# Audio tower on one core: the token mixer's convolution of chunks one to three, interleaved in pairs of heads

## The chip, the cores and the metric

The kernel runs on one core of one Trainium2 chip. The metric is the device time of one launch in microseconds, lower is better. In the trace PE is TensorE (PEld its weight loads), DVE VectorE, ACT ScalarE, POOL GpSimd, SP SyncE.

## What is computed

A layer of an audio tower on 2,048 rows of 1,024 channels (32 sequences of 64 rows, after folding four steps of 256 channels into one row), in three parts. The change lies in the first, the token mixer:

```
h = xf @ W_proj + b_proj                 # 1024 x 1024
y = layernorm(h, ln_g, ln_b)
w = softmax((y @ W_wgen + b_wgen) by head over 5 taps)       # 8 heads
conv = sum over taps k of  w[.., k] * y shifted by 4-k rows  # per head, 128 channels
out = h + relu(conv @ W_ff + b_ff)
```

Then follow `h + attention(layernorm(h))` (8 heads of 64, causal) and `h + ffn(layernorm(h))` (16 heads, 64 to 256 to 64, with a permutation of channels).

## The kernel before

**Layout.** The rows (tokens) are the columns of work here, cut into CH = 4 chunks of N = 512. Channels lie on the 128 partitions in KB = 8 blocks; a chunk's block is 128x512. Every engine has its program written out by hand, and semaphores order the engines (`since(e, s, c, per, k)` waits until semaphore `s` has reached `c * per + k`). Each engine runs its program in order. All eight PSUM banks (128x512 f32 each) are in use.

**The feed-forward product** of chunk c, `conv @ W_ff`, is done by `ff_group(c, g, k)`: for the output blocks of group g (`A_GROUPS`: banks 0 1 2, then 3 4 5, then 6 7) and the input block k, three matmuls each (high and low halves: `split3`, lines 339 to 341). Group 2 is thus eight steps of six matmuls into banks 6 and 7. I call such a step G0 to G7.

**The convolution** of a chunk is done head by head, between those steps of the chunk ahead of it. `turn(n, h)` (T0 to T7) is four PE transposes of the head's y into bank 0 or 2, by h % 2 (line 1687). ACT copies it to SBUF (`turn_evac`, line 900), into one of two buffers. `conv(n, h)` (C0 to C7) is 32 small 64x64 matmuls with the head's band of tap weights (line 1706), into two banks. DVE prepares the band (`band_turn`, line 1320; two buffers). ACT takes the result's high part (`conv_high`, line 905), DVE the low part (`conv_low`, line 1326), which releases the banks. For chunks 1 to 3 every head uses the same two banks, 3 and 4, so `conv(n, h)` waits for the low part of head h-1 (`cv_lo`).

**PE's order in `b_step(c)`**, c = 0, 1, 2, after groups 0 and 1 of chunk c: T0 | G0 T1 C0 | G1 T2 C1 | ... | G6 T7 C6 | G7 C7, where G are of chunk c and T and C of chunk c + 1.

**Beside it, in chunk 1's convolution only** (c = 0), ACT squares the eight blocks of the last chunk's centred values for its layernorm, one square after each `conv_high` (line 364; S0 to S7). ACT's order there is: copy of T(h), high part of C(h-1), S(h). The squares have two buffers, and S(k) waits for POOL's variance addition k-2 (`ln_square_act` waits on `ln_vac`, for k from 2). POOL's order, written out by hand, is:

```
for m in range(3):
    b_add(0, m)
for k in range(1, 4):
    ln_var_add(g, CH - 1, k)
for m in range(3, 6):
    b_add(0, m)
for k in range(4, KB):
    ln_var_add(g, CH - 1, k)
```

`ln_var_add(k)` (line 375; V1 to V7) needs S(k). `b_add(0, m)` (line 768) adds the residual block m, which SP loads into two buffers: the load of block m + 2 is issued after addition m and its store (lines 581, 585).

Of the kernel before, what the change touches and what calls it, by code (L numbers as in the profile page):

```python
# [10 lines left out]
KB = D // P  # L11
# [22 lines left out]
def audio_tower(nc, x_t, w_proj, w_ff, w_gen, w_qkv_t, w_o_t, up, down, vecs, perm, *outs):  # L34
# [12 lines left out]
    with ctx:  # L47
# [5 lines left out]
        def sem(name):  # L53
            return ctx.enter_context(nc.semaphore(name))
# [140 lines left out]
        cv_mm, cv_hi, cv_lo, ff_mm, ff_ev, ff_add = (  # L195
            sem(s) for s in ("cv_mm", "cv_hi", "cv_lo", "ff_mm", "ff_ev", "ff_add"))
# [20 lines left out]
        def since(e, s, c, per, k):  # L217

            if isinstance(c, int):
                if c * per + k > 0:  # L220
                    e.wait_ge(s, c * per + k)
            else:
                e.wait_ge(s, c * per + k)
# [50 lines left out]
        def cv_out(n, h, s):  # L274

            return bank[cv_banks(n, h)[s]][:, 0:N // 2].rearrange("p (t q) -> p t q", q=SEQ)
# [73 lines left out]
        def ln_mean_pe(pe, L):  # L350
            since(pe, ln_sum, L, 7, 7)
            since(pe, ln_std, L - 1, 1, 1)
            pe.matmul(bank[LN_BANK][:, :], mean_w[:, :], acc[:, :], start=True, stop=True).then_inc(ln_mean, 1)
# [28 lines left out]
        def ln_var_pe(pe, L):  # L382
            since(pe, ln_vac, L, 7, 7)
            since(pe, ln_d, L, 8, 8)
            pe.matmul(bank[LN_BANK][:, :], mean_w[:, :], vacc[:, :], start=True, stop=True).then_inc(ln_var, 1)
# [1202 lines left out]
        def _(pe):  # L1588
# [62 lines left out]
            def gate_block(n, k):  # L1651
                since(pe, yr_lo, n, 8, k + 1)
                if k == 0 and n < CH - 1:
                    pe.wait_ge(a_ev, 8 * (n + 1))
                if k == 0 and n == CH - 1:
                    pe.wait_ge(ff_ev, 8)

                for whole in (True, False) if k == 0 else (False, True):
                    if whole:
                        mm = pe.matmul(bank[7][0:2 * LOGITS, :], wg[:, k, :, :], yr_h[:, k % 2, :],  # L1660
                                       start=k == 0, stop=k == KB - 1)
                    else:
                        mm = pe.matmul(bank[7][0:LOGITS, :], wg[:, k, 0, :], yr_l[:, k % 2, :],
                                       start=False, stop=False)
                mm.then_inc(yr_used, 1)

            def gate_turn(n):

                since(pe, lg_ev, n, 1, 1)
                for t in range(TILES):  # L1670
                    mm = pe.matmul(bank[7][:, t * LOGITS:(t + 1) * LOGITS],
                                   lg[:, t * P:(t + 1) * P], fold[0:2 * LOGITS, :], start=True, stop=True)
                mm.then_inc(lgt_mm, 1)

            def turn(n, h):

                pe.wait_ge(y_b, 8 * n + h + 1)
                if h < 2:
                    if n == 0:
                        pe.wait_ge(a_ev, 8 * (CH - 1) + YT_BANKS[1] + 1)  # L1680
                    else:
                        pe.wait_ge(ff_ev, 8 * (n - 1) + YT_BANKS[h] + 1)
                else:
                    pe.wait_ge(yt_ev, 8 * n + h - 1)
                y = db[n]
                for t in range(TILES):
                    mm = pe.transpose(bank[YT_BANKS[h % 2]][:, t * P:(t + 1) * P], y[:, h, t * P:(t + 1) * P],  # L1687
                                      ident[:, :])
                mm.then_inc(yt_mm, 1)

            def conv(n, h):
                if n == 0:
                    pe.wait_ge(a_ev, 8 * (CH - 1) + cv_banks(n, h)[1] + 1 + (h == 0))
                    since(pe, cv_lo, n, 8, h - 1)
                elif h == 0:
                    pe.wait_ge(ff_ev, 8 * (n - 1) + CV_BANKS[0][1] + 1)
                else:
                    pe.wait_ge(cv_lo, 8 * n + h)
                since(pe, yt_ev, n, 8, h + 1)
                since(pe, ar_ev, n, 8, h + 1)  # L1700
                halves = [slice(SEQ * i, SEQ * i + SEQ) for i in range(2)]
                for t in range(TILES):
                    for f in range(2):
                        col = t * P + f * SEQ
                        for s in range(2):
                            mm = pe.matmul(bank[cv_banks(n, h)[s]][halves[f], t * SEQ:(t + 1) * SEQ],  # L1706
                                           yt[halves[s], h % 2, col:col + SEQ],
                                           ar[halves[s], h % 2, t * SEQ:(t + 1) * SEQ], start=True, stop=True)
                mm.then_inc(cv_mm, 1)

            def ff_group(c, g, k):
                ms = A_GROUPS[g]
                if g == 0:
                    since(pe, cv_lo, c, 8, k + 1)
                if isinstance(c, int) and c == 0 and g < 2:
                    wait_units(pe, U_FF + KB * g + k + 1)
                for m in ms:
                    cols = slice(m * P, (m + 1) * P)
                    mm = split3(pe, bank[m][:, :], (wf_h[:, k, cols], wf_l[:, k, cols]),
                                (cv_h[:, k, :], cv_l[:, k, :]), k == 0, k == KB - 1)  # L1720
                    if k == KB - 1:
                        mm.then_inc(ff_mm, 1)
                if g == 2 and c == CH - 1 and k < KB - 1:
                    mm.then_inc(ff_used, 1)

            def b_step(c, ahead):


                LATE = CH - 1
                for i in range(2 * KB):  # L1730
                    if c == 0 and i == KB:
                        pe.wait_ge(mean3_ok, 1)
                    if c == 1 and i == 1:
                        pe.wait_ge(ff_ev, 8)
                        ln_var_pe(pe, LATE)
                    if not ahead and i == 2:
                        pe.wait_ge(ff_ev, 8 * (CH - 1))
                        ln_mean_pe(pe, CH)
                    if not ahead and i == 9:
                        ln_var_pe(pe, CH)  # L1740
                    ff_group(c, i // KB, i % KB)
                    if c == 1 and 0 <= i - 5 < KB:
                        gate_block(LATE, i - 5)
                    if c == 1 and i == 14:
                        gate_turn(LATE)
                if ahead:
                    turn(c + 1, 0)
                if c == 1:
                    pe.wait_ge(ln_std, CH)
                    pe.wait_ge(sm5, 8 * LATE + 1)  # L1750
                elif ahead:
                    pe.wait_ge(ff_ev, 8 * c)
                else:
                    pe.wait_ge(ln_std, CH + 1)
                for k in range(KB):
                    ff_group(c, 2, k)
                    if ahead:
                        if k + 1 < KB:
                            turn(c + 1, k + 1)
                        conv(c + 1, k)  # L1760


# [3 lines left out]
            for h in range(CONV_HEADS):  # L1766
                if h + 1 < CONV_HEADS:
                    turn(0, h + 1)
                conv(0, h)
                if h == MEAN_AFTER:  # L1770
                    stat_mean_pe(pe, CH - 1, MEAN_BANK)
            for c in range(CH - 1):
                b_step(c, True)
            b_step(CH - 1, False)


# [210 lines left out]
            for s in range(CH * KB):  # L1987
                c, a = divmod(s, KB)
# [14 lines left out]

A_GROUPS = [(0, 1, 2), (3, 4, 5), (6, 7)]

YT_BANKS, CV_BANKS = (0, 2), ((3, 4), (6, 7))

SMALL_AFTER, LOAD_AFTER, FIRST_LOW = 2, 4, 6

# [25 lines left out]

def cv_banks(n, h):

    return CV_BANKS[h % 2 if n == 0 else 0]


# [38 lines left out]
```

## Time and profile before

| | us |
|---|---|
| median of 3 runs | 966.39 (962.8 to 966.87) |
| the profiled execution: its time | 968.3 |
| its span, first to last instruction | 965.9 |
| mean granted TensorE clock | 0.991 of full |
| PE busy | 943.1 |
| chunk 1's convolution (T0 to the end of C7) | 256.9 to 278.1 |
| chunk 2's | 316.5 to 337.6 |
| chunk 3's | 370.4 to 391.5 |

A line of the timeline gives the start, the length (of the union, where several like instructions are merged, xN), the engine, the line of the kernel, the operation and its tiles, and in brackets the idle time of the engine before it with what released it. PE records overlap, because the matmuls are pipelined: how fast PE goes is read from the distance of starts, not from lengths.

### The profile page before, as it was taken

What the parts mean: (1) busy time and instruction counts of PE and PEld (TensorE: products, weight loads), DVE (VectorE), ACT (ScalarE), POOL (GpSimd) and SP (SyncE); (2) the same over time, 40 slices, a digit from 0 to 9 for tenths busy, and PEclk for the clock granted to TensorE, in tenths of its full rate; (3) what the DMA queues carried; (4) which work ended last, traced back from release to release, by engine and by line L of the source; (5) the groups of instructions that cost most, each with busy time, mean ns of one, the idle gap of its engine ahead of it and who ended that gap; (6) DMA issues with size and microseconds to landing.
All of it is one profiled execution on the core that took longest, in us unless ns stands there. A gap on an engine that the chain in (4) does not pass through costs nothing.

```text
span 965.9 us, 15776 instructions
## 1 busy us (share of the span) xinstructions
PE 943.1 (98%) x6108; PEld 707.5 (73%) x6108; DVE 540.3 (56%) x887; ACT 438.3 (45%) x774; POOL 387.6 (40%) x312
## 2 busy tenths in 40 slices
PE   9999999998999999999999999999999999999996
PEld 8778787776877788788778878878887766623342
DVE  5254544878658312356475266257064479788773
ACT  6244444482754543436253243244132232287874
POOL 1224242523752221823560550451023157487742
PEclk9999999999999999999999999999999999999999
DMA  7750605128354254149002002100124985634521
GB/s 259 279 177 1 224 1 211 33 92 257 115 181 125 88 150 161 45 160 336 5 12 99 22 12 61 60 13 23 42 79 143 259 302 201 260 116 137 170 105 76
DMA packets 54383, 122.99 MB, mean 127 GB/s; under 512 B 16283, under 2 KB 17307, under 8 KB 49830
## 3 DMA queue, kind: packets, MB, share of 16 engines
q1 hardware_dynamic: 49190, 105.22, 32.7%
q0 software_dynamic: 5120, 16.78, 5.1%
q8 instruction: 48, 0.79, 0.3%
q14 instruction: 25, 0.20, 0.1%
HBM read 79.37 MB, written 42.60 MB: 126 GB/s over the span
## 4 chain that ended last, share of the span: by engine, by line
PE 79%; DVE 6%; DMA 6%; issue 3%; POOL 2%; ACT 2%; SPq 1%; POOLq 0%; DVEq 0%; ACTq 0%
PE bank L339 20%; PE bank L341 19%; PE bank L340 19%; PE bank L1978 6%; PE bank L1962 3%; PE bank L1706 2%; DMA h<-h_s 2%; PE bank L1687 1%; DVE h L1489 1%; DVE sq L420 1%; DMA stage<-w_proj 1%; PE bank L1965 1%; DMA stage<-w_ff 1%; PE bank L1863 1%; PE bank L1836 1%
## 5 line engine op out<-in xcount | busy, mean ns | idle before, releaser
L375 POOL TENSOR_TENSOR vacc<-vacc,sq 128x512 f32<-128x512 f32 x72 | 97.4, 1353 | 44.9 <-ACT sq L425 33.3
L339 PE MATMUL bank<-cv_h,wf_h 128*128 128x512 f32 x256 | 105.2, 411 | 3.2 <-POOL wf_l L333 3.2
L339 PE MATMUL bank<-xa_h,wp_h 128*128 128x512 f32 x256 | 102.5, 400 | 0.1
L341 PE MATMUL bank<-cv_h,wf_l 128*128 128x512 f32 x256 | 100.5, 393 | 0.0
L340 PE MATMUL bank<-cv_l,wf_h 128*128 128x512 f32 x256 | 100.5, 392 | 0.0
L341 PE MATMUL bank<-xa_h,wp_l 128*128 128x512 f32 x256 | 100.4, 392 | 0.0
L340 PE MATMUL bank<-xa_l,wp_h 128*128 128x512 f32 x256 | 100.3, 392 | 0.0
L768 POOL TENSOR_TENSOR fo<-fo,res 128x512 f32<-128x512 f32 x32 | 44.1, 1392 | 100.2 <-ACT fo L910 75.2
L1170 ACT ACTIVATE gt<-bank 128x512 f32<-128x512 f32 x128 | 66.0, 603 | 33.6 <-PE bank L1962 20.1
L1978 PE MATMUL bank<-gt,dn_f 128*64 128x512 f32 x256 | 61.8, 604 | 0.0
L425 ACT ACTIVATE sq<-sq 128x512 f32<-128x512 f32 x56 | 34.6, 637 | 59.7 <-DVE sq L420 59.7
L1400 DVE TENSOR_SCALAR qk<-bank,vec 128x256 f32<-128x256 f32 x32 | 14.0, 480 | 84.1 <-PE bank L341 84.1
L339 PEld LDWEIGHTS bank<-cv_h,wf_h 128*128 128x128 f32 x256 | 48.4, 189 | 15.6 <-issue 4.5
L339 PE MATMUL bank<-vs_h,wo_h 128*128 128x512 f32 x128 | 53.1, 415 | 4.4 <-DVE vs_l L1449 4.0
L1326 DVE TENSOR_TENSOR cv_l<-bank,cv_h 128x256 fp32r<-128x256 f32 x64 | 24.2, 420 | 59.1 <-ACT cv_h L905 58.7
L403 POOL TENSOR_TENSOR acc<-acc,ho 128x512 f32<-128x512 f32 x24 | 33.6, 1399 | 58.9 <-ACT ho L881 56.6
L339 PEld LDWEIGHTS bank<-xa_h,wp_h 128*128 128x128 f32 x256 | 48.4, 189 | 11.9 <-issue 0.7
L340 PEld LDWEIGHTS bank<-xa_l,wp_h 128*128 128x128 f32 x256 | 48.5, 190 | 10.7 <-issue 0.7
L341 PEld LDWEIGHTS bank<-cv_h,wf_l 128*128 128x128 f32 x256 | 48.4, 189 | 10.5
L341 PEld LDWEIGHTS bank<-xa_h,wp_l 128*128 128x128 f32 x256 | 48.4, 189 | 10.4
L340 PEld LDWEIGHTS bank<-cv_l,wf_h 128*128 128x128 f32 x256 | 48.5, 190 | 10.1 <-issue 1.0
L833 POOL DMA_INDIRECT out<-hg,rows x32 | 37.3, 1165 | 42.1 <-DVE hg L1568 39.3
(194 smaller groups left out, 2240.2 us busy)
## 6 DMA issues: line engine op xcount, KB each, us to landing
xs<-x_t SPq DMA_DIRECT2D x32, 256.0 KB, 6.1
h_s<-ho SPq DMA_DIRECT2D x8, 1024.0 KB, 4.3
res<-h_s SPq DMA_DIRECT2D x32, 256.0 KB, 3.6
h_s<-fo SPq DMA_DIRECT2D x32, 256.0 KB, 2.5
dc<-h_s SPq DMA_DIRECT2D x4, 2048.0 KB, 9.0
h<-h_s SPq DMA_DIRECT2D x8, 1024.0 KB, 10.7
h_s<-h SPq DMA_DIRECT2D x8, 1024.0 KB, 6.1
band_s<-zero SPq DMA_DIRECT2D x4, 1096.0 KB, 8.5
```

The lines of the kernel that those rows point to most:

```text
L339: pe.matmul(o, wh, xh, start=start, stop=False)
L340: pe.matmul(o, wh, xl, start=False, stop=False)
L341: return pe.matmul(o, wl, xh, start=False, stop=stop)
L375: g.tensor_tensor(vacc[:, :], t[:, 0, :] if k == 1 else vacc[:, :], t[:, at, :], ALU.add).then_inc(ln_vac, 1)
L403: g.tensor_tensor(acc[:, :], blk(0) if k == 1 else acc[:, :], blk(k), ALU.add).then_inc(ln_sum, 1)
L425: act.activation(d, d, ACT.Square).then_inc(ln_sq, 1)
L768: g.tensor_tensor(fo[m % 4][:, :], fo[m % 4][:, :], res[:, m % 2, :], ALU.add).then_inc(ff_add, 1)
L833: g.indirect_dma_start(out=outs[c], out_offset=bass.IndirectOffsetOnAxis(ap=rows[:, k:k + 1], axis=0), in_=hg[c % 3][:, k, :], in_offset=N ...
L1170: act.activation(gt[a % 2][:, i, :], bank[i][:, :], ACT.Gelu).then_inc(gelu_ok, 1)
L1326: ins = v.tensor_tensor(one_seq(cv_l[:, h, :], s), cv_out(n, h, s), one_seq(cv_h[:, h, :].bitcast(F32), s), ALU.subtract)
L1962: mm = pe.matmul(bank[2 * blk + j][:, :], up_f[r, a, cols], dd[r, a, :], start=True, stop=True)
L1978: pe.matmul(bank[4 + a % 2][side, :], dn_f[:, FFB * a + 2 * head + blk, :], gt[a % 2][:, i, :], start=blk == 0, stop=blk == 1).then_inc(g_ ...
```

## The change

For chunks 1 to 3 the order in `b_step` becomes T0 T1 | G0 G1 T2 T3 C0 C1 | G2 G3 T4 T5 C2 C3 | G4 G5 T6 C4 C5 | G6 T7 C6 | G7 C7. Heads 1, 3 and 5 get banks 1 and 5 (free since group 2 writes only 6 and 7); the other heads keep 3 and 4. The waits of `conv` follow: C0 and C1 wait for the relu that empties their banks, C2 to C6 for the low part of head h-2, C7 for that of head 6. ACT's, DVE's, POOL's and SP's programs are unchanged.

```diff
@@ conv(n, h)
-                elif h == 0:
-                    pe.wait_ge(ff_ev, 8 * (n - 1) + CV_BANKS[0][1] + 1)
+                elif h < 2:
+                    pe.wait_ge(ff_ev, 8 * (n - 1) + cv_banks(n, h)[1] + 1)
+                elif h < 7:
+                    pe.wait_ge(cv_lo, 8 * n + h - 1)
                 else:
                     pe.wait_ge(cv_lo, 8 * n + h)
@@ b_step(c, ahead)
                 if ahead:
                     turn(c + 1, 0)
+                    turn(c + 1, 1)
...
                 for k in range(KB):
                     ff_group(c, 2, k)
-                    if ahead:
-                        if k + 1 < KB:
-                            turn(c + 1, k + 1)
+                    if ahead and k < 6 and k % 2:
+                        for h in (k + 1, k + 2):
+                            if h < 7:
+                                turn(c + 1, h)
+                        conv(c + 1, k - 1)
+                        conv(c + 1, k)
+                    if ahead and k == 6:
+                        turn(c + 1, 7)
+                    if ahead and k >= 6:
                         conv(c + 1, k)
@@ module level
-YT_BANKS, CV_BANKS = (0, 2), ((3, 4), (6, 7))
+YT_BANKS, CV_BANKS = (0, 2), ((3, 4), (6, 7), (1, 5))
@@ cv_banks(n, h)
-    return CV_BANKS[h % 2 if n == 0 else 0]
+    return CV_BANKS[h % 2 if n == 0 else 2 if h % 2 and h < 6 else 0]
```

## Rows read from the trace of the kernel before

**Rows 1.** The page: engines' busy time, and the chain that ended last.

```profile
PE 943.1 (98%) x6108; PEld 707.5 (73%) x6108; DVE 540.3 (56%) x887; ACT 438.3 (45%) x774; POOL 387.6 (40%) x312
...
PE 79%; DVE 6%; DMA 6%; issue 3%; POOL 2%; ACT 2%; SPq 1%; POOLq 0%; DVEq 0%; ACTq 0%
```

**Rows 2.** Timeline of PE, chunk 1's convolution (start, length, engine, line).

```profile
256.23 0.39 PE L339 MATMUL bank<-cv_h,wf_h 128*128 128x512 f32 x1
...
256.92 0.60 PE L1687 MATMUL bank<-ident,db_next 128*128 128x128 f32 x4
...
258.74 0.60 PE L1687 MATMUL bank<-ident,db_next 128*128 128x128 f32 x4
...
262.54 0.50 PE L339 MATMUL bank<-cv_h,wf_h 128*128 128x512 f32 x1
...
264.04 0.60 PE L1687 MATMUL bank<-ident,db_next 128*128 128x128 f32 x4
264.57 0.69 PE L1706 MATMUL bank<-ar,yt 64*64 64x64 f32 x32
265.19 0.50 PE L339 MATMUL bank<-cv_h,wf_h 128*128 128x512 f32 x1
...
277.46 0.69 PE L1706 MATMUL bank<-ar,yt 64*64 64x64 f32 x32
```

**Rows 3.** Timeline of PE, chunk 3's convolution: T1 and C7.

```profile
372.21 0.60 PE L1687 MATMUL bank<-ident,db_late 128*128 128x128 f32 x4
...
390.83 0.69 PE L1706 MATMUL bank<-ar,yt 64*64 64x64 f32 x32
```

**Rows 4.** Timeline of PE, chunk 0: T0 and T1 back to back.

```profile
206.58 1.03 PE L1687 MATMUL bank<-ident,db 128*128 128x128 f32 x8
```

**Rows 5.** Timeline of PE, attention: two sets of 32 small matmuls back to back.

```profile
497.14 0.69 PE L1863 MATMUL bank<-pt,vv 64*64 64x64 f32 x32
497.66 0.65 PE L1836 MATMUL bank<-qk 64*64 64x64 f32 x32
498.24 0.50 PE L339 MATMUL bank<-xc_h,wq_h 128*128 128x512 f32 x1
```

**Rows 6.** Timeline of ACT, POOL and DVE, chunk 1's convolution from S3 on.

```profile
265.87 0.64 ACT L364 ACTIVATE sq<-db_late 128x512 f32<-128x512 f32 x1
266.59 1.39 POOL L375 TENSOR_TENSOR vacc<-vacc,sq 128x512 f32<-128x512 f32 x1 [1.26 <-ACT sq L364]
267.93 2.73 POOL L768 TENSOR_TENSOR fo<-fo,res 128x512 f32<-128x512 f32 x2
272.61 1.28 POOL L768 TENSOR_TENSOR fo<-fo,res 128x512 f32<-128x512 f32 x1 [1.95 <-DMA res<-h_s]
273.85 5.59 POOL L375 TENSOR_TENSOR vacc<-vacc,sq 128x512 f32<-128x512 f32 x4
275.23 0.63 ACT L364 ACTIVATE sq<-db_late 128x512 f32<-128x512 f32 x1 [1.31 <-POOL vacc L375]
276.65 0.76 DVE L1326 TENSOR_TENSOR cv_l<-bank,cv_h 128x256 fp32r<-128x256 f32 x2 [1.25 <-ACT cv_h L905]
```

**Rows 7.** Timeline of PE: three gaps elsewhere in the kernel.

```profile
217.69 0.69 PE L1706 MATMUL bank<-ar,yt 64*64 64x64 f32 x32 [1.08 <-DVE ar L1320]
...
234.87 0.77 PE L339 MATMUL bank<-cv_h,wf_h 128*128 128x512 f32 x1 [3.17 <-POOL wf_l L333]
...
783.82 0.47 PE L339 MATMUL bank<-vs_h,wo_h 128*128 128x512 f32 x1 [1.90 <-DVE vs_l L1449]
```

**Rows 8.** Windows: engines' busy us (instructions), then granted PE clock, DMA share, GB/s.

```profile
216.00:220.00 4.00, 2.92 (x70) 2.15 (x71) 3.35 (x9) 2.46 (x7) 0.00 (x0) 1.00 0.20 66
234.00:239.00 5.00, 4.13 (x11) 3.31 (x12) 5.00 (x4) 1.28 (x3) 5.00 (x4) 0.66 0.97 217
784.00:788.00 4.00, 4.00 (x12) 3.11 (x11) 3.79 (x7) 0.31 (x1) 3.08 (x4) 0.57 0.64 186
```

**Rows 9.** Waits in total: POOL for residual loads (us, times, longest).

```profile
POOL fo L768 <- DMA res<-h_s: 25.0, 9, 6.6
```

## The prediction, made before the changed kernel was run

> **What bounds the kernel now.** I read the page first: PE is busy for 943.1 of 965.9 us, and the chain that ended last runs through PE for 79% of the span [rows 1]. So a microsecond taken from PE's own sequence counts, and a microsecond in which PE is made to wait counts too. Then I read PE's timeline through the three stretches that the diff touches. A plain matmul of a group is 0.23 us behind the one before it: three of them from 256.23 to T0 at 256.92. A full turn of the loop, from the first matmul of one G to that of the next, is 2.65 us (262.54 to 265.19), of which G is 1.50, T until C starts 0.53, and C until the next G 0.62. T0 with all of G0 behind it is 1.82 (256.92 to 258.74) [rows 2]. From T1 to C7 chunk 3 takes 18.62 us, seven turns of 2.65 and 0.07 for the way into C7: nothing waits there [rows 3]. In chunk 1 it is 18.72 (258.74 to 277.46) [rows 2], so C7 already waits 0.1 us. Last I read the other engines beside chunk 1, because only there ACT's squares stand in the same queue as the copies that PE needs.
>
> **What PE's sequence saves.** Per merged pair of heads, one change from T to C and one from C to G go away, and nothing is removed from the work.
> - *Two groups in a row:* the second has six matmuls at 0.23, 1.38 us, instead of 1.50. G G is 2.88.
> - *Two turns in a row:* eight transposes take 1.03 where four take 0.60 [rows 4, 2], so the second T costs 0.43, and T T is 0.53 + 0.43 = 0.96.
> - *Two products in a row:* no row of before shows C C. The nearest is attention, where a set of 32 small matmuls of the same tile follows another at once: 497.14 to 498.24, 1.10 us for both, against 0.62 for one [rows 5, 2]. The second costs 0.48. Its bounds are 0.62 (no gain: each C as dear as today) and 0.47, the start-to-start distance if nothing at all is lost. I take 0.48, since those rows have the same count and tile, other banks for the second set, and three waits ahead of it like C.
>
> A pair is 2.88 + 0.96 + 1.10 = 4.94 against 2 x 2.65 = 5.30: 0.36 saved (0.22 with the dear C). Three pairs are merged in each chunk: T2 T3 C0 C1; T4 T5 C2 C3; T6 C4 C5. T0 T1 ahead of G0 only moves 0.43 us from one place to another. So PE's sequence is 3 x 0.36 = 1.08 us shorter per chunk, 3.2 us in three (2.0 with the dear C).
>
> The Trainium skill ("TensorE: Matmul & The Clock Gate", the section on 56 ns against 53.3 ns) says that starts of matmuls never come closer than about 25 ns however small they are. By that floor 32 products would take 0.80 us, a second C would cost 0.80, and by an estimate from it a pair would save 0.04 us, 0.4 us in nine. The trace does not agree: 32 products and the way out take 0.62 [rows 2], so the rows decide.
>
> **Do the waits hold?** In chunks 2 and 3 ACT has only copies between the pairs, so yes: C(h) now waits for the low part of head h-2, a whole pair older, and T2 to T5 for copies made a pair earlier. Bank 5's relu is done before ACT copies T0, since it stands ahead of it in ACT's queue. C0 comes later than now, so DVE's bands are there. Both chunks get their 1.08 us.
>
> **Chunk 1 is another matter.** There every square S(h) stands behind the high part of C(h-1), and C2 moves. On PE: T0 256.92; T2 at +1.82 +0.43 +1.38 = 260.55; C0 +0.96 = 261.51; G2 +1.10 = 262.61; T4 +2.88 = 265.49; C2 +0.96 = 266.45. Today C2 is at 264.57: it comes 1.88 us later. What hangs on it today: S3 at 265.87 (1.30 behind C2), V3 at 266.59, the two residual additions 3 and 4 at 267.93, addition 5 at 272.61, which waited 1.95 us for a residual block whose load SP issues only after addition 3, then V4 to V7 from 273.85, 1.40 each, and S6 at 275.23, which stood 1.31 us waiting for V4 [rows 6]. Behind S6 in ACT's queue come the copy of T7 and the high part of C6, then DVE's low part, 276.65 to 277.41, then C7 at 277.46 [rows 6, 2]. Every link is back to back or a fixed latency, with no slack, apart from POOL's 1.26 us ahead of V3, which is itself the wait for S3. So the 1.88 us pass through to C7: 279.34.
>
> ACT can't take S6 earlier, and nothing that is behind it can pass. On PE, C7 would be due at: G4 266.45 + 1.10 = 267.55; T6 270.43; C4 270.96; G6 272.06; T7 273.56; C6 274.09; G7 274.71; C7 + 1.57 = 276.28. So PE stands still for about 3.0 us, with nothing to do: what is queued behind C7 is group 0 of chunk 1, which is not let past it. Chunk 1 ends 1.88 us later instead of 1.08 earlier.
>
> The earlier pairs of chunk 1 hold. From C0 at 261.51 ACT goes through the high part of C0, S1, copy of T2, high part of C1, S2, copy of T3 at about 0.54 each from 262.27 (S3 stands 1.30 behind its C and the high part 0.54 before it), so the copy of T3 ends near 265.6, and T5, which needs its bank, is due at 265.92.
>
> **The clock.** A gap of 3 us may cost more than its length. After the gap of 3.17 us ahead of 234.87 and that of 1.90 ahead of 783.82 the granted clock fell to its lower level (1.2 of 2.4 GHz): it was 0.66 over 234 to 239 and 0.57 over 784 to 788, which is 5 x 0.34 and 4 x 0.43, 1.7 us of full-rate work lost each time. After the gap of 1.08 ahead of 217.69 it stayed at 1.00 [rows 7, 8]. Mine is as long as those that fell, with dense matmuls ahead of it, so I take 1.7 (bounds 0 and 1.7).
>
> **Sum.** Chunk 1 +1.88 + 1.7, chunks 2 and 3 -2.16: +1.4 us. The later parts follow PE, whose gaps in them are waits for other engines that PE itself releases, so a shift passes on whole. Against the profiled execution, 968.3, that is 969.7; the median of the runs is 1.9 below the profiled one, so 966.4 + 1.4 = 967.8. A change of 0.5% (4.8 us) is about what this measurement can tell from none, and mine is 0.15%.
>
> **Rivals.**
> 1. *The stall is there, the clock holds.* For it: C7 and the work before are dense, and part of the half-rate stretch may fall into the gap itself. Against: both gaps of 1.9 us and more lost the full 1.7. Net +1.88 - 2.16 = -0.3: 966.1. Chance 0.2.
> 2. *No stall: the pairs give all they promise.* It would need the wait of addition 5 for its residual (1.95 us) or ACT's for V4 (1.31) to shrink by what C2 is later. For it: a load that is in flight alone may land sooner. Against: the load is issued by what it waits for. Then -3.2: 963.2, and with the dear C 964.4. Chance 0.14.
> 3. *Slower by more than can be missed.* The load of residual 5, issued between additions 3 and 4, may land much later than now, since it moves into other traffic. The longest wait of POOL for such a load is 6.6 us against 1.95 here [rows 9, 6]: C7 would be 4.65 later still, net +6.1: 972.5. It decides from a wait of 5.4 us on, where +4.8 is reached. Against: SP has nothing else in flight at that point. Chance 0.05.
> 4. *Small waits at each pair* (T5 misses its 0.3 us of margin, or a C waits for a band): 0.1 to 0.3 each, 967 to 969; inside the forecast's own width. The forecast with these has 0.61.
>
> **The numbers.** Forecast 967.8, its own range 966.5 to 969.5. Rivals 1 and 2 lie below it, so the range reaches down to 963.0; above it ends at 970.3, short of rival 3. Against no change (966.4): faster needs below 961.6, which no case reaches but for the scatter of the runs (962.8 to 966.9 before): 0.04. Slower needs above 971.2, rival 3 and scatter: 0.06. The same: 0.9.
>
> **What the profile after would show.** In chunks 2 and 3, from T0 to C7 19.4 us instead of 20.4, with C C 1.10 and T T 0.96: that proves the saving. In chunk 1, V3 near 268.5, S6 near 277.1 waiting for V4, a PE gap of about 3 us ahead of C7 near 279.3, put down to DVE's low part, and a granted clock below 1 behind it. C C at 1.24 would show the dear C. If C7 of chunk 1 starts near 276.3, the chain through POOL was wrong. If C7 is late but the clock stays at 1.00, only the price of the gap was.

## The result and the profile after

The changed kernel takes 970.33 us (968.0 to 972.9, 10 runs) against 965.44 (962.7 to 966.9, 10 runs on the same chips): a ratio of 1.0054, 95% interval 1.0040 to 1.0068. It is slower, by 4.9 us, where I forecast +1.4 us and a range that ended at 970.3. The profiled execution took 970.1 us with a span of 968.2.

The page after, in the lines that answer to [rows 1]:

```profile
PE 937.9 (97%) x6108; PEld 705.3 (73%) x6108; DVE 541.7 (56%) x887; ACT 435.4 (45%) x774; POOL 386.7 (40%) x312
...
PE 81%; DVE 6%; DMA 4%; issue 3%; POOL 3%; ACT 2%; SPq 1%; POOLq 0%; DVEq 0%; ACTq 0%
```

PE is busy for 5.2 us less in a span that is 2.3 us longer: the same 6,108 instructions take less of its time, and waits came. First chunk 3, where nothing else stands in the way (timeline of PE; to be held against [rows 3]):

```profile
373.45 1.03 PE L1687 MATMUL bank<-ident,db_late 128*128 128x128 f32 x8
377.06 1.04 PE L1687 MATMUL bank<-ident,db_late 128*128 128x128 f32 x8
378.03 1.16 PE L1708 MATMUL bank<-ar,yt 64*64 64x64 f32 x64
382.02 1.03 PE L1687 MATMUL bank<-ident,db_late 128*128 128x128 f32 x8
...
392.79 0.69 PE L1708 MATMUL bank<-ar,yt 64*64 64x64 f32 x32
```

T0 of chunk 3 in the kernel before, for the comparison:

```profile
370.38 0.60 PE L1687 MATMUL bank<-ident,db_late 128*128 128x128 f32 x4
```

T T and C C are merged records now. From T2 (377.06) to T4 (382.02) is 4.96 us, where two turns of the loop took 5.30. From T0 to C7 is 392.79 - 373.45 = 19.34 us, against 390.83 - 370.38 = 20.45 before. Chunk 2 reads the same, 19.35 against 20.46. So each gives back 1.11 us.

Then chunk 1, first PE (timeline, to be held against [rows 2]):

```profile
255.37 1.03 PE L1687 MATMUL bank<-ident,db_next 128*128 128x128 f32 x8
...
259.95 1.16 PE L1708 MATMUL bank<-ar,yt 64*64 64x64 f32 x64
...
263.94 0.60 PE L1687 MATMUL bank<-ident,db_next 128*128 128x128 f32 x4
264.74 0.63 PE L1687 MATMUL bank<-ident,db_next 128*128 128x128 f32 x4 [0.20 <-ACT yt L900]
265.30 1.16 PE L1708 MATMUL bank<-ar,yt 64*64 64x64 f32 x64
...
279.56 1.13 PE L1708 MATMUL bank<-ar,yt 64*64 64x64 f32 x32 [4.26 <-DVE cv_l L1326]
280.63 0.79 PE L339 MATMUL bank<-cv_h,wf_h 128*128 128x512 f32 x1
281.22 0.63 PE L340 MATMUL bank<-cv_l,wf_h 128*128 128x512 f32 x1
```

PE stands still for 4.26 us ahead of C7, and C7 itself takes 1.07 us from its start to the next plain matmul instead of 0.62. From T0 to C7 it is 24.19 us instead of 20.54. The queues beside it (timeline of ACT, POOL, DVE and SP, against [rows 6]):

```profile
263.48 0.63 ACT L364 ACTIVATE sq<-db_late 128x512 f32<-128x512 f32 x1 [0.55 <-POOL vacc L375]
...
267.31 1.41 POOL L375 TENSOR_TENSOR vacc<-vacc,sq 128x512 f32<-128x512 f32 x1 [1.86 <-ACT sq L364]
...
268.69 2.69 POOL L768 TENSOR_TENSOR fo<-fo,res 128x512 f32<-128x512 f32 x2
...
270.36 0.43 SPq L581 DMA_DIRECT2D res<-h_s  x1
...
274.75 1.27 POOL L768 TENSOR_TENSOR fo<-fo,res 128x512 f32<-128x512 f32 x1 [3.38 <-DMA res<-h_s]
275.98 5.49 POOL L375 TENSOR_TENSOR vacc<-vacc,sq 128x512 f32<-128x512 f32 x4
...
277.33 0.63 ACT L364 ACTIVATE sq<-db_late 128x512 f32<-128x512 f32 x1 [4.54 <-POOL vacc L375]
...
278.75 0.76 DVE L1326 TENSOR_TENSOR cv_l<-bank,cv_h 128x256 fp32r<-128x256 f32 x2 [5.11 <-ACT cv_h L905]
```

The chain is the forecast one, link by link: V3, additions 3 and 4, the load of residual 5, addition 5, V4, S6, the copy of T7, the high part of C6, its low part, C7. Two links are longer than forecast. POOL waits 3.38 us for the load instead of 1.95. And C2 is 0.4 us later than drawn (9.93 us behind T0, forecast 9.53), since S2 waited 0.55 us for V1 and the copy that T5 needs stands behind S2: from T4 to C2 is 1.36 us instead of 0.96.

The clock in windows (columns as in [rows 8]):

```profile
274.00:277.00 3.00, 1.31 (x6) 0.73 (x4) 0.00 (x0) 0.00 (x0) 2.25 (x2) 1.00 0.15 54
277.00:284.00 7.00, 4.43 (x40) 3.64 (x41) 1.51 (x4) 5.28 (x10) 6.51 (x6) 0.53 0.27 93
284.00:290.00 6.00, 6.00 (x25) 4.57 (x25) 3.74 (x2) 0.69 (x1) 0.00 (x0) 0.98 0.86 293
```

From 277.4, still inside the gap, to 284.2 the granted clock is at its lower level (0.5 of full), twice as long as behind the two gaps of [rows 7] after which it fell. From C7 to T0 of chunk 2 it takes 41.14 us (279.56 to 320.70) against 39.06 before (277.46 to 316.52). T0 of chunk 2, before and then after:

```profile
316.52 0.60 PE L1687 MATMUL bank<-ident,db_next 128*128 128x128 f32 x4
```

```profile
320.70 1.04 PE L1687 MATMUL bank<-ident,db_next 128*128 128x128 f32 x8
```

The 2.08 us are the clock's: in six of the seven experiments below in which it stays at 1.00 here, three with pairs in chunk 1 and three without, the same stretch takes 39.06 or 39.07 us again.

### The profile page after: what moved, and what is told of

The parts are those of the page before. It is cut to its first block, busy times and chain, and to the rows that moved or that the text cites. A ratio compares the mean times of both kernels' runs of the same rounds, so it can differ in the third digit from the quotient of the medians.

```text
span 968.2 us, 15776 instructions
## 1 busy us (share of the span) xinstructions
PE 937.9 (97%) x6108; PEld 705.3 (73%) x6108; DVE 541.7 (56%) x887; ACT 435.4 (45%) x774; POOL 386.7 (40%) x312
## 4 chain that ended last, share of the span: by engine, by line
PE 81%; DVE 6%; DMA 4%; issue 3%; POOL 3%; ACT 2%; SPq 1%; POOLq 0%; DVEq 0%; ACTq 0%
PE bank L339 21%; PE bank L340 20%; PE bank L341 20%; PE bank L1987 6%; PE bank L1971 3%; DMA stage<-w_proj 2%; PE bank L1708 2%; DVE sq L420 1%; PE bank L1687 1%; DMA stage<-w_ff 1%; PE bank L1974 1%; DVE h L1489 1%; PE bank L1872 1%; DMA res<-h_s 1%; PE bank L1845 1%
```

## The experiments

All ratios are to the kernel before, timed on the same chip, with 95% intervals. My theory was that the whole loss is chunk 1's chain through POOL and the clock behind it.

**Pairs in chunks 2 and 3 only.** A table of chunks decides in `conv`, `cv_banks` and `b_step`:

```diff
+PAIRED = (2, 3)
-    return CV_BANKS[h % 2 if n == 0 else 2 if h % 2 and h < 6 else 0]
+    return CV_BANKS[h % 2 if n == 0 else 2 if n in PAIRED and h % 2 and h < 6 else 0]
```

> The changed kernel with pairs in chunks 2 and 3 only; chunk 1 keeps the order and banks of before. Theory A (all of the loss is chunk 1's wait for C7 and the clock behind it): 2.2 us faster than before (2 x 1.11, as the changed kernel's trace shows for these chunks), ratio 0.9977, no PE gap of over 0.5 us ahead of a C7, chunk 1's T0 to C7 20.5 us. Rival B (the pairs cost something in later stages too): as slow as before or slower.

Measured: 0.9990 (0.9977 to 1.0002), 963.73 us against 964.34. Chunk 1 takes 20.45 us from T0 to C7, chunks 2 and 3 19.34 each, and no C7 waits. The 2.2 us are there in the profile; the timed runs show between 2.2 less and 0.2 more, so they bear the theory out only at their edge. POOL's wait for residual 5 here, with chunk 1 as before:

```profile
271.44 1.28 POOL L768 TENSOR_TENSOR fo<-fo,res 128x512 f32<-128x512 f32 x1 [1.84 <-DMA res<-h_s]
```

**Pairs in chunk 1 only**, the same edit with `PAIRED = (1,)`.

> The changed kernel with pairs in chunk 1 only. Theory A: slower than before by the whole of chunk 1's part, 5 to 7 us (5.3 in the profile from T0 of chunk 1 to T0 of chunk 2, and the changed kernel's 4.9 plus the 2.2 that chunks 2 and 3 give), ratio 1.005 to 1.007; a gap of 3 to 5 us ahead of C7 and a granted clock of 0.5 behind it. Rival B: about half of the changed kernel's loss.

Measured: 1.0047 (1.0029 to 1.0065), 969.33 us against 964.34. T0 to C7 of chunk 1 is 23.91 us; from T0 of chunk 1 to T0 of chunk 2 it is 65.48, 5.88 more than before. Chunk 1 alone makes the loss, and in the profile more than the changed kernel's. The timed runs say 2.8 to 6.3 us, so they reach only the lower part of the 5 to 7 us expected. The two parts taken singly, 0.9990 and 1.0047, add up to less than the 1.0054 of both, by no more than the intervals allow.

```profile
278.75 1.14 PE L1708 MATMUL bank<-ar,yt 64*64 64x64 f32 x32 [3.96 <-DVE cv_l L1326]
```

**Addition 5 behind V4 to V7.** Nothing else moves:

```diff
-            for m in range(3, 6):
+            for m in range(3, 5):
                 b_add(0, m)
             for k in range(4, KB):
                 ln_var_add(g, CH - 1, k)
-            for m in range(6, KB):
+            for m in range(5, KB):
                 b_add(0, m)
```

> The changed kernel, with one move in POOL's program: the residual addition 5 goes behind the variance additions V4 to V7, so V4 no longer waits for the residual load of 3.4 us; additions 3 and 4 stay ahead of V4. Theory A: V4 starts near 3 us behind V3's end instead of 7.3, S6 finds it done, C7's gap goes (under 0.7 us), the clock stays at 1.00, and the kernel is about 3 us faster than before (-3.2 at best), 7 to 8 faster than the changed one. Rival C (C7 is held by ACT's queue itself, copies and squares in bursts, not by POOL): the gap stays at 2 us or more.

Measured: 0.9975 (0.9960 to 0.9990), 962.22 us. The gap is gone: T0 to C7 is 19.89 us. POOL and then PE (two timelines of this kernel):

```profile
270.30 5.58 POOL L375 TENSOR_TENSOR vacc<-vacc,sq 128x512 f32<-128x512 f32 x4
```

```profile
274.23 0.70 PE L1708 MATMUL bank<-ar,yt 64*64 64x64 f32 x32
```

V4 starts 4.0 us behind V3 (266.29), C7 waits for nothing, and the granted clock is 1.00 from 274 to 290. So addition 5 with its residual load in front of V4 made the gap, and ACT's queue by itself did not. By the ratio it is 2.4 us faster than before, where I had expected about 3. One small wait stands in the profile behind it: PE waits 0.36 us at 306.38 for the last chunk's low part, and T0 to T0 is 59.60 us, no better than before (39.71 us from C7 on instead of 39.06). The reason for that wait was not tried.

**POOL's order written anew**: additions 3, 4 and 5 go into the waits ahead of V1, V2 and V3.

```diff
-            for m in range(3):
+            for m in range(4):
                 b_add(0, m)
-            for k in range(1, 4):
-                ln_var_add(g, CH - 1, k)
-            for m in range(3, 6):
-                b_add(0, m)
-            for k in range(4, KB):
+            ln_var_add(g, CH - 1, 1)
+            b_add(0, 4)
+            ln_var_add(g, CH - 1, 2)
+            b_add(0, 5)
+            for k in range(3, KB):
                 ln_var_add(g, CH - 1, k)
```

> The changed kernel with POOL's order add3, V1, add4, V2, add5, V3 to V7, so that additions 3 to 5 stand in the time in which POOL waits for squares, and neither additions nor the residual load stand ahead of V4. Theory A: as the kernel with addition 5 moved or 0.2 us better, -3 us against before. Rival C: the gap ahead of C7 stays at 2 us or more. A third way: addition 4 or 5 waits for its load and delays V2 or V3, then a copy ahead of T5 or C4 is late and a gap of 0.5 to 2 us opens there instead.

Measured: 0.9968 (0.9953 to 0.9982), 961.32 us against 964.34: 3.0 us faster than before, where the changed kernel is 4.9 slower. T0 to C7 of chunk 1 is 19.74 us, T0 to T0 58.80, and C7 waits for nothing.

**The changed kernel once more.**

> The changed kernel once more, for a second profile of it beside the others on this chip. Theory A: ratio 1.004 to 1.007 again; chunk 1's T0 to C7 between 22.4 us (if the load of residual 5 lands as fast as in the profile of before, 1.95 us of waiting) and 26 us, and the gap ahead of C7 moves one for one with POOL's wait for that load (3.38 us of waiting gave a gap of 4.26).

Measured: 1.0054 (1.0031 to 1.0076), the same ratio. T0 to C7 23.99 us, the gap 4.01:

```profile
276.04 1.28 POOL L768 TENSOR_TENSOR fo<-fo,res 128x512 f32<-128x512 f32 x1 [3.15 <-DMA res<-h_s]
...
280.86 1.13 PE L1708 MATMUL bank<-ar,yt 64*64 64x64 f32 x32 [4.01 <-DVE cv_l L1326]
```

POOL waits 0.23 us less than in the first profile, the gap is 0.25 shorter: one for one.

**PE kept busy in the gap.** The 14 matmuls compute nothing that is used:

```diff
                 for k in range(KB):
                     ff_group(c, 2, k)
+                    if c == 0 and k == 7:
+                        pe.wait_ge(cv_lo, 8 * (c + 1) + 6)
+                        for i in range(14):
+                            pe.matmul(bank[1][:, :], wf_h[:, 0, 0:P], wf_h[:, 0, 0:N], start=True, stop=True)
```

> The changed kernel, with 14 matmuls of 128x512 (0.23 us each, 3.2 us) put between G7 and C7 of chunk 1, into bank 1, which is free there; they compute nothing that is used. PE is busy in the gap, and C7 starts no sooner. If the clock behind the gap costs what the windows say (2.1 us from C7 to the next T0, 0.4 in C7 itself), the granted clock stays at 1.00 and the kernel is 2 to 2.5 us faster than the changed one, 2.5 to 4 slower than before (ratio about 1.003). If the loss is the gap alone, it is as slow as the changed one.

Measured: 1.0023 (1.0006 to 1.0039), 966.66 us against 965.18. C7 starts no sooner, 23.99 us behind T0 as in the kernel it is made from, but T0 to T0 is 63.05 us instead of 65.31 (timeline, then the window, of this kernel):

```profile
274.35 3.33 PE L1763 MATMUL bank<-wf_h 128*128 128x512 f32 x14
278.53 0.69 PE L1708 MATMUL bank<-ar,yt 64*64 64x64 f32 x32 [0.84 <-DVE cv_l L1326]
```

```profile
274.00:284.00 10.00, 9.15 (x68) 6.94 (x67) 2.38 (x5) 5.97 (x11) 8.54 (x7) 1.00 0.29 97
```

The clock stays at 1.00, and 2.26 us come back in the profile, about 3 in the timed runs (whose intervals, 1.0006 to 1.0039 and 1.0031 to 1.0076, overlap a little). Idle work is faster here than idleness.

**POOL's new order in the kernel before**, with its single heads.

> The kernel before, with POOL's new order alone (add3, V1, add4, V2, add5, V3 to V7). Theory A: next to nothing, since C7 waited 0.1 us in chunk 1 before: 0 to -0.3 us, ratio 0.999 to 1.001; S6 no longer waits. Rival D (the new order of POOL brings its gain by itself, with or without pairs): about -3 us, ratio 0.997.

Measured: 1.0006 (0.9993 to 1.0019). T0 to C7 20.45 us. The order gives nothing by itself; it only frees the pairs.

**ACT's order too.** In chunk 1 ACT copies T(h+1) ahead of S(h), on top of POOL's new order:

```diff
-                    if ahead and h < CONV_HEADS:
+                    if ahead and h < CONV_HEADS and not (first and 0 < h < 7):
                         turn_evac(c + 1, h)
...
+                    if first and h < 6:
+                        turn_evac(c + 1, h + 1)
                     if first and h < CONV_HEADS:
                         ln_square_act(act, CH - 1, h, db_late[:, LATE_ORDER[h], :])
```

> The changed kernel with POOL's new order, and in chunk 1 ACT copies T(h+1) ahead of square S(h) for h up to 5, so that no copy that a pair's second transpose needs stands behind a square that waits for V1. Theory A: T5's wait of 0.20 us goes, chunk 1's T0 to C7 is 19.35 us as in chunks 2 and 3 (19.74 with POOL's order alone), -3.3 us against before, ratio 0.9965. If the squares now come too late for V4 to V7, C7 or the variance matmul behind it waits 0.3 to 1 us and nothing is won.

Measured: 0.9973 (0.9955 to 0.9991), 961.94 us against 965.18. The last wait is gone: T0 to C7 19.29 us, T0 to T0 58.36, a span of 958.8, the shortest of all profiles. Part of that is luck: this is the only profile in which the clock did not fall behind the gap near 235 us, a stretch that cost each of the others 1.7 us or more of full-rate work. The runs can't tell it from the kernel without the edit (0.9968).

**The load ahead of the store**, in the changed kernel:

```diff
+                    if c == 0 and m == 3:
+                        res_load(c, m + 2)
                     ff_store(c, m)
...
-                    if m + 2 < KB:
+                    if m + 2 < KB and (c, m) != (0, 3):
                         res_load(c, m + 2)
```

> The changed kernel, with one swap in SP's program: the load of residual 5 is issued ahead of the store of block 3 instead of behind it, 0.36 us sooner and with no store of its own ahead of it on the queue. In five profiles with pairs in chunk 1 POOL waited 3.1 to 3.4 us for this load (it started 4.1 to 4.4 us behind the issue of the load), in two without 1.8 to 1.95 (2.9 to 3.0). Theory A: the gap ahead of C7 shrinks by what the load comes sooner: 0.4 us if the store is not to blame, 1.5 us or more if the load was slow because of the store. The clock still falls, so the ratio stays at 1.003 to 1.005. If the gap does not shrink with POOL's wait, the chain is wrong.

Measured: 1.0039 (1.0022 to 1.0057), 969.75 us against 964.85. POOL's wait goes from 3.15 or 3.38 to 1.82 us and the gap from 4.01 or 4.26 to 3.02 (timeline of POOL, then of PE):

```profile
276.49 1.58 POOL L770 TENSOR_TENSOR fo<-fo,res 128x512 f32<-128x512 f32 x1 [1.82 <-DMA res<-h_s]
```

```profile
281.62 1.09 PE L1710 MATMUL bank<-ar,yt 64*64 64x64 f32 x32 [3.02 <-DVE cv_l L1328]
```

Of the 1.3 to 1.6 us only 0.36 are the earlier issue; the rest is a faster landing (addition 5 starts 3.20 us behind the issue instead of 4.17 or 4.39) once the store is not ahead of it. The gap shrinks by 0.3 us less than the wait, because addition 5 itself takes 1.58 us here instead of 1.28. The half-rate stretch is shorter too, about 3.4 us, and from T0 to T0 it is 63.53 us. It is a third lever on the same chain, though the timed runs can't tell this kernel from the changed one (1.0054). What the swap does not show is that the store by itself makes the load slow. In the kernels without pairs in chunk 1 the load was issued behind the same store in the same way, and addition 5 started 2.87 to 3.04 us behind the issue.

**Pairs in the same two banks**, in chunks 2 and 3 only (the edit is to the kernel of the first experiment):

```diff
-                elif h < (2 if n in PAIRED else 1):
+                elif h < 1:
                     pe.wait_ge(ff_ev, 8 * (n - 1) + cv_banks(n, h)[1] + 1)
-                elif n in PAIRED and h < 7:
+                elif False:
                     pe.wait_ge(cv_lo, 8 * n + h - 1)
...
-    return CV_BANKS[h % 2 if n == 0 else 2 if n in PAIRED and h % 2 and h < 6 else 0]
+    return CV_BANKS[h % 2 if n == 0 else 0]
```

> Pairs in chunks 2 and 3 only, but both heads of a pair in banks 3 and 4, so the second product waits for the low part of the first. From start to start of two products 2.0 us instead of 0.48 (0.76 until ACT starts, 0.42 and 0.76 until DVE has the low part), 1.5 us more for each of six pairs: chunks 2 and 3 take 19.35 + 4.5 = 23.9 us from T0 to C7, and the kernel is 6.9 us slower than before, ratio 1.007, more if the clock falls in such gaps. If the pairs need no banks of their own (rival: a product's low part is done by then), it is as fast as the kernel with pairs in chunks 2 and 3, 0.998.

Measured: 1.0060 (1.0036 to 1.0084), 970.95 us against 964.85. Chunks 2 and 3 take 23.90 and 23.89 us, as worked out:

```profile
325.40 0.69 PE L1708 MATMUL bank<-ar,yt 64*64 64x64 f32 x32
327.39 0.69 PE L1708 MATMUL bank<-ar,yt 64*64 64x64 f32 x32 [1.29 <-DVE cv_l L1326]
```

The second product starts 1.99 us behind the first instead of 0.48, six times. The banks of their own are what makes pairs pay at all. The clock stays at 1.00 through all six gaps of 1.29 us.

The stretches side by side, from the profiles' timelines of PE (us):

| kernel | gap ahead of C7, chunk 1 | T0 to C7, chunk 1 | T0 of chunk 1 to T0 of chunk 2 | chunk 3, T0 to C7 | ratio to before |
|---|---|---|---|---|---|
| before | none listed | 20.54 | 59.60 | 20.45 | 1 |
| changed | 4.26 | 24.19 | 65.33 | 19.34 | 1.0054 |
| changed, once more | 4.01 | 23.99 | 65.31 | 19.35 | 1.0054 |
| pairs in chunks 2, 3 | none | 20.45 | 59.51 | 19.34 | 0.9990 |
| pairs in chunk 1 | 3.96 | 23.91 | 65.48 | 20.45 | 1.0047 |
| addition 5 moved | none | 19.89 | 59.60 | 19.34 | 0.9975 |
| POOL's order | none | 19.74 | 58.80 | 19.35 | 0.9968 |
| matmuls in the gap | 0.84 | 23.99 | 63.05 | 19.34 | 1.0023 |
| POOL's order in the kernel before | none | 20.45 | 59.52 | 20.45 | 1.0006 |
| POOL's and ACT's order | none | 19.29 | 58.36 | 19.35 | 0.9973 |
| load ahead of store | 3.02 | 22.96 | 63.53 | 19.34 | 1.0039 |
| pairs in the same banks, chunks 2, 3 | none | 20.60 | 59.66 | 23.89 | 1.0060 |

## Why the prediction was wrong, step by step

- **What PE's sequence saves: right.** 1.08 us per chunk forecast, 1.11 measured in chunks 2 and 3. In chunk 1 it is 0.65 to 0.80 with POOL's chain freed alone, and 1.16 to 1.25 with ACT's order changed too (19.29 us against 20.45 and 20.54). The second product costs 0.48 us as read from attention [rows 5]: 64 products in one record of 1.16, after T T of 1.03. From a record of 32 products (0.69 us) to one of 64 (1.16) it is 0.47 us, or 15 ns for each further product. The Trainium skill's page "TensorE: Matmul & The Clock Gate" has matmul starts never closer than about 25 ns; for these 64x64 products the trace does not agree, by the 15 ns just worked out.
- **That the waits hold in chunks 2 and 3: right.** No gap in either.
- **The chain in chunk 1: right in every link, wrong in two lengths.** Forecast T0 to C7 22.42 us, measured 24.19 and 23.99. The step that failed is the one that says that "the 1.88 us pass through to C7" and nothing is added.
  - 1.43 us are the load of residual 5, whose wait I took over as 1.95 from one profile (3.38 and 3.15 measured). It was rival 3 in kind, to which I gave 0.05. Its case against, that SP has nothing else in flight, does not hold: the stores of blocks 3 and 4 and the next load are on the same queue. But they were there before too, at the same distances, so they alone are not the reason.
  - 0.4 us are "the earlier pairs of chunk 1 hold". I laid ACT's slots end to end and forgot that S2, like S3, waits for V1 (the rule "k-2, for k from 2" given above reads in the code as `max(1, k - 2)`), and POOL starts V1 only behind S1. T5 then waits for a copy behind S2.
- **The clock: right that it falls, wrong in size.** I took 1.7 us, with 1.7 as the upper bound, from gaps of 1.9 and 3.17 us. It was low for 6.8 us instead of about 3.4, of which 4.6 fell on work: 2.08 us from C7 to T0 by the trace, 2.26 from T0 to T0 by the kernel with matmuls in the gap. The length of the gap is not all that decides. In the kernel with pairs in chunks 2 and 3 a gap of 3.22 us, near 233 us, ahead of the same matmul as the 3.17 us of [rows 7], also brought the clock down for 6.8 us.
- **Sum.** With what the profile shows: chunk 1 3.65 + 2.08, chunks 2 and 3 -2.22, together +3.5 instead of +1.4. The medians say +4.9 and, the second time, +5.0 (by the ratio 3.9 to 6.6 us and 3.0 to 7.3). What is left, 1.4 us, lies just outside the first interval and inside the second; it is not explained. In the second measurement the mean granted clock of the timed runs is 0.9896 against 0.9935 before, 3.8 us of full-rate work, and chunk 1's stretch holds 3.4 of them; that leaves little for a clock lost elsewhere.
- **The base, and luck.** The profile of before, 968.3 us, is longer than each of the ten timed executions (median 965.4). The clock falls in it near 32, 784 and 811 us, where the profile of the kernel before with POOL's new order (span 961.5) keeps it high. The falls near 32 and 784 cost about 2 and 1.6 us. The one near 811 costs next to nothing in the span: where it is missing, PE waits for other engines near 840 instead (0.9 and 1.2 us in the changed kernel's profile). I took 966.4, the median of three executions, as the base, 1.0 us above the median of ten, and by luck that brought the forecast nearer to 970.33 than its +1.4 deserved.
- **Open too:** why the load of residual 5 lands 1.2 us later with pairs in chunk 1 (4.09 to 4.39 us from its issue to addition 5 in four profiles, against 2.87, 2.98 and 3.04 without). The swap with the store shows that with pairs the order of the two matters. What else differs between them is not shown.
- **The range.** It ended at 970.3, 0.03 below the median. It was tied to rival 3's start rather than to a sum of two bounds that hang together: a longer wait for the load makes the gap longer, and the longer gap can make the clock's price higher.

## What to carry to other kernels

Before work is made to run in bursts on the bound engine, follow what the burst delays: here three engines' fixed orders and a load turned 2.3 us of delay in one product into a gap of 4.3 and a fallen clock, while the merging itself paid nearly what the rows said. Where such a chain holds the bound engine, break it at its cheapest link, which was an addition in POOL's list that nothing was waiting for yet; that turned 0.5% slower into 0.25 to 0.3% faster. And a link that is a DMA landing is no constant (this one started its addition 2.87 to 4.39 us behind the issue): price it from its spread, and price gap and clock together.

## What the runs showed of the hardware that I had not expected

- After the three PE gaps of 4.0 to 4.3 us in chunk 1 the granted clock fell inside the gap and stayed at its lower level for 6.8 us in all; after the one of 3.0 us it was low for about half as long. With 14 unused matmuls in the gap, leaving 0.84 us idle, it did not fall.
- Gaps of one length do not always cost the same. At 232 to 237 us all twelve profiles have a gap of 2.8 to 3.7 us: behind it the clock was low for 3.4 us in ten, for 6.8 us in one (gap 3.22) and not at all in one (gap 3.20). Near 784 us all have a gap of 1.9 us, and the clock fell behind it in seven; near 811 us again 1.9 us, and it fell in eight.
- What such a fall costs depends on what follows. Near 784 us, from one gap to the next is 27.6 us with it and 26.0 without. Near 811 us, from the gap to the end of the span is 154.1 to 154.9 us with it and 153.5 to 154.8 without.
- With pairs in chunk 1, a 256 KB load issued 0.36 us behind a 256 KB store on the same queue landed about 1 us later than one issued ahead of it (addition 5 at 4.17 or 4.39 us behind the issue against 3.20). Without the pairs it was issued behind the same store and landed early all the same (2.87 to 3.04).
